# Gate logits from one product with 16 weight columns: rounded weights and their rest side by side, summed after the turn

## What is computed

```python
def _L0_ffn_ref(x, gamma1, Wq, bq, Wdown, bdown, Wup, bup, Wo, bo, gamma2, Wg, bg, We):
    ...
    x = x + (out @ Wo + bo)
    h2 = _rmsnorm(x, gamma2)
    gate = jax.nn.softmax(h2 @ Wg + bg, axis=-1)
    combined = jnp.einsum('btd,edf,bte->btf', h2, We, gate)
    return x + combined
x = L0_attn_hidden_states
x = x + 0.5 * _L0_ffn_ref(_layernorm(x, axis=-1), ...)
x = x + _L0_attn_ref(_layernorm(x, axis=-1), ...)
x = x + 0.5 * _L0_ffn_ref(_layernorm(x, axis=-1), ...)
```

## Time and profile before

| | us |
|---|---|
| median of 3 runs | 1097.27 |
| lowest and highest | 1095.72, 1097.42 |
| the profiled execution | 1095.98 |
| its span in the trace | 1094.1 |
| PE busy | 1030.9 (94%) |
| DVE busy | 872.0 (80%) |
| POOL busy | 726.5 (66%) |
| ACT busy | 653.4 (60%) |

### The profile page before, as it was taken

The page is one execution under the profiler, slowest core; times in us unless marked ns, Lnnn a source line. Parts: engine busy times, 40 slices in busy tenths (PEclk is TensorE's granted clock), DMA queues, the critical chain, the costliest instruction groups (busy, mean ns, idle before and its releaser), DMA issues. The chain is left out here.

```text
span 1094.1 us, 28463 instructions
## 1 busy us (share of the span) xinstructions
PE 1030.9 (94%) x11320; PEld 779.6 (71%) x11320; DVE 872.0 (80%) x1372; ACT 653.4 (60%) x1331; POOL 726.5 (66%) x727
## 2 busy tenths in 40 slices
PE   4799999999999989999999999877999999999997
PEld 3577878888888755666656565456878788788785
DVE  7888788788786379899899999977886777876853
ACT  4565465564665357777777776645655555655642
POOL 8677476576564458787787778983674664755544
PEclk9899999999999999999999999998999999999999
DMA  6210000000000000000000000000000000000000
GB/s 198 69 40 1 1 2 1 2 1 2 2 2 1 2 1 1 2 1 2 1 2 1 2 2 1 2 1 2 2 2 21 21 2 20 22 1 22 21 1 40
DMA packets 8411, 14.30 MB, mean 13 GB/s; under 512 B 2516, under 2 KB 6102, under 8 KB 8280
## 3 DMA queue, kind: packets, MB, share of 16 engines
q1 hardware_dynamic: 8280, 12.47, 3.4%
HBM read 8.28 MB, written 4.19 MB: 11 GB/s over the span
## 5 line engine op out<-in xcount | busy, mean ns | idle before, releaser
L441 PE MATMUL psum<-we,h 128*128 128x512 f32 x1536 | 396.6, 402 | 0.3 <-DVE X L1059 0.3
L441 PEld LDWEIGHTS psum<-we,h 128*128 128x128 f32 x1536 | 275.9, 188 | 59.3 <-issue 2.3
L1237 ACT ACTIVATE late<-psum,gate 128x256 f32<-128x256 f32 x256 | 107.2, 471 | 140.7 <-PE psum L441 96.1
L1413 POOL TENSOR_TENSOR late<-late 128x512 f32<-128x512 f32 x64 | 82.5, 1290 | 147.8 <-ACT late L1237 147.8
L1085 DVE TENSOR_REDUCE oT<-psum 128x128 fp32r<-128x1024 f32 x128 | 155.7, 1219 | 26.3 <-PE psum L808 26.2
L1059 DVE SCALAR_TENSOR_TENSOR X<-psum,gate,X 128x256 f32<-128x256 f32 x256 | 122.8, 480 | 60.1 <-PE psum L441 47.9
L1287 ACT ACTIVATE kvx<-psum 128x1024 f32<-128x1024 f32 x128 | 131.2, 1025 | 65.0 <-PE psum L818 62.5
L1450 POOL TENSOR_TENSOR kvx<-kvx,late 128x2048 f32<-128x2048 f32 x32 | 124.6, 3894 | 42.1 <-ACT late L1294 42.1
L1091 DVE TENSOR_REDUCE late<-kvx 128x256 f32<-128x2048 f32 x64 | 145.7, 2277 | 0.0
L1450 POOL TENSOR_TENSOR late<-kvx,late 128x2048 f32<-128x2048 f32 x32 | 124.5, 3891 | 24.7 <-ACT late L1294 24.7
L818 PE MATMUL psum<-oT,neg_id 128*128 128x512 f32 x256 | 93.8, 447 | 12.6 <-DVE oT L1085 12.1
(11 more groups left out here) (152 smaller groups left out, 1979.0 us busy)
## 6 DMA issues: line engine op xcount, KB each, us to landing
X<-in_L_attn_hidden_states SPq DMA_DIRECT2D x8, 512.0 KB, 5.3
out<-X SPq DMA_DIRECT2D x8, 512.0 KB, 2.6
X<-in_L_ffn_We SPq DMA_DIRECT2D x2, 1024.0 KB, 9.8
kvx<-in_L_ffn_Wq SPq DMA_DIRECT2D x1, 256.0 KB, 3.2
kvx<-in_L_ffn_Wup SPq DMA_DIRECT2D x2, 128.0 KB, 3.1
kvx<-in_L_ffn_Wo SPq DMA_DIRECT2D x1, 256.0 KB, 4.2
X<-in_L_attn_Wk SPq DMA_DIRECT2D x1, 256.0 KB, 2.8
X<-in_L_attn_Wq SPq DMA_DIRECT2D x1, 256.0 KB, 3.5
```

The lines of the kernel that those rows point to most:

```text
L441: ins = e.matmul(out_ap, l, r, start=(n == 0 and not opened), stop=(n == len(terms) - 1), skip_group_check=opened)
L1237: e.activation(y[:, n // 2 * 2 + w, :], psum[:, u % 3, w * D:(w + 1) * D], ACT.Copy, scale=gate[k % 2][:, i, 2 * n + w:2 * n + w + 1]).the ...
L1413: own.step(e.tensor_tensor(y[:, 0:2, :], y[:, 0:2, :], y[:, 2:4, :], ALU.add))
```

## The change

The weights' rounded part and their rest are laid side by side as 16 stationary columns (`wg` is now 128 x KC x 2 x 8). One product of the 16 columns with h2's rounded part and one with h2's rest, for two blocks of features, are four matmuls where six were; the product of rest by rest is computed as well. The result is 16 rows: 8 with the rounded weights, 8 with their rest. gate_copy copies 16 rows; the bias is added to the first 8 and zero to the others, for which POOL clears the bias tile first, and SP waits for that clearing before it loads the bias. gateT turns 16 rows, and gate_sub has one step more: DVE adds the two halves from PSUM into `gl` in SBUF, and maximum and subtraction then read `gl`. In the planner's table two lengths are changed.

```diff
@@ all_steps @@
-            put("PE", size(1400, 720), ("gate", s, w), *(("h2_lo", s, p) for p in own), turned, ("rest_lo", 5))
+            put("PE", size(950, 490), ("gate", s, w), *(("h2_lo", s, p) for p in own), turned, ("rest_lo", 5))
             put("ACT", size(680, 430), ("gate_copy", s, w), ("gate", s, w))
             put("PE", size(300, 200), ("gateT", s, w), ("gate_copy", s, w), last)
-            put("DVE", size(400, 350), ("gate_sub", s, w), ("gateT", s, w))
+            put("DVE", size(650, 600), ("gate_sub", s, w), ("gateT", s, w))
@@ macaron, tiles @@
-        wg = sbt(ctx, "wg", [P, 2, KC, E], F32R)
+        wg = sbt(ctx, "wg", [P, KC, 2, E], F32R)
-        bgate = sbt(ctx, "bgate", [E, 1])
+        bgate = sbt(ctx, "bgate", [2 * E, 1])
-        gT = ct[0:E].rearrange("e g n -> e (g n)")
+        gT = ct[0:2 * E].rearrange("e g n -> e (g n)")
@@ pe_program @@
-                    terms = [(wg[:, y_, kk, :], h2[k % 2][:, x_, kk, cols]) for kk in range(KC) for x_, y_ in THREE]
-                    product(e, psum[0:E, b, cols], terms).then_inc(s_gl, 1)
+                    terms = [(wg[:, kk, :, :].rearrange("p w e -> p (w e)"), h2[k % 2][:, x_, kk, cols]) for kk in range(KC) for x_ in range(2)]
+                    product(e, psum[0:2 * E, b, cols], terms).then_inc(s_gl, 1)
-                        ins = e.transpose(psum[:, b, i * E:(i + 1) * E], gT[:, i * P:(i + 1) * P], ident[0:E, 0:E])
+                        ins = e.transpose(psum[:, b, 2 * i * E:2 * (i + 1) * E], gT[:, i * P:(i + 1) * P], ident[0:2 * E, 0:2 * E])
@@ dve_program, gate_sub @@
-                    pg = psum[:, b, span(tiles, E)].rearrange("p (i e) -> p i e", e=E)
+                    both = psum[:, b, span(tiles, 2 * E)].rearrange("p (i w e) -> p i e w", w=2, e=E)
+                    pg = gl[:, own_t, :]
                     if done(k, piece[2]) > 1:
                         e.wait_ge(s_gate, done(k, piece[2]) - 1)
                     e.wait_ge(s_gTT, done(k, piece[2]))
+                    own.step(e.tensor_reduce(pg, both, AX.X, ALU.add))
+                    e.wait_ge(own.sem, own.n)
                     own.step(e.tensor_reduce(gs[:, 0, own_t], pg, AX.X, ALU.max))
                     e.wait_ge(own.sem, own.n)
-                    e.tensor_tensor(gl[:, own_t, :], pg, gs[:, 0, own_t].unsqueeze(2).to_broadcast([P, n, E]),
+                    e.tensor_tensor(pg, pg, gs[:, 0, own_t].unsqueeze(2).to_broadcast([P, n, E]),
                                     ALU.subtract).then_inc(s_gsub, 1)
@@ act_program @@
-                    split_hi(wg[:, 0], raw_g, l_wg, 16)
+                    split_hi(wg[:, :, 0], raw_g, l_wg, 16)
-                    e.activation(gT[:, cols], psum[0:E, b, cols], ACT.Identity, bias=bgate[:, 0:1]).then_inc(s_gT, 1)
+                    e.activation(gT[:, cols], psum[0:2 * E, b, cols], ACT.Identity, bias=bgate[:, 0:1]).then_inc(s_gT, 1)
@@ pool_program @@
             own.step(e.memset(half_neg[:, :], -0.5))
+            own.step(e.memset(bgate[:, :], 0.0))
             e.memset(ones2f, 1.0).then_inc(s_const, 1)
-                    rest_lo(wg[:, 1], raw_g, wg[:, 0], l_wg, 6)
+                    rest_lo(wg[:, :, 1], raw_g, wg[:, :, 0], l_wg, 6)
@@ sp_program @@
-            e.dma_start(bgate[:, :], a["L0_ffn_bg"].rearrange("(n o) -> n o", o=1)).then_inc(l_bgate, 16)
+            e.wait_ge(s_const, 2)
+            e.dma_start(bgate[0:E, :], a["L0_ffn_bg"].rearrange("(n o) -> n o", o=1)).then_inc(l_bgate, 16)
```

## The result

| | before | after |
|---|---|---|
| median, us | 1097.35 (4 runs) | 1104.45 (4 runs) |
| ratio, 95% interval | | 1.0068 [1.005, 1.0085] |
| a second comparison, us | 1097.34 (15 runs) | 1102.93 (5 runs) |
| its ratio | | 1.0052 [1.0037, 1.0066] |
| span of the profiled execution, us | 1094.1 | 1103.0 |

A forecast was written before the change was run, and what follows sets the result against it. The prediction took TensorE, busy 1030.9 of 1094.1 us (94%), as the bound. Its terms, 0.8 + 2.5 + 1.8 - 1.05 - 1.6 + 0.2 = 2.65 us off the median of 1097.27, gave 1094.6 us, range 1091.0 to 1098.2.

The follow-up runs named there:

- e3: The kernel after, with DVE's halving step in gate_soft taken out and its factor 0.5 put into the last step: 1101.15 us, 1.0030 against the kernel before.
- e4: The kernel after, with ScalarE's exp of the gates put ahead of its copy of turned probabilities: 1102.17 us, 1.0041 against the kernel before.

## What to carry to other kernels

When a short step of DVE moves in time, look up what POOL runs at its new place: here a multiplication or subtraction with its operands in SBUF, begun while POOL's instruction ran, lasted until that ended, however small it was. Its wait is not shown as idle time but inside its own duration. A step whose duration differs between like stages is the sign to look for. Where such a step stands in a chain that PE waits for, fewer steps, an operand in PSUM or a reduction in its place can be worth more than a faster product: here one folded multiplication gave 2.3 us alone, and about 6 with the smaller product, which alone gave none. And lengths in a planner's table are a change of their own: test the new arithmetic in the old order first.

## What the runs showed of the hardware

- A DVE multiplication of 128x4 took 0.17 us beside no POOL instruction and 1.19 us beside a POOL addition of 1.28 us, ending within 0.03 us of it. The next step did the same when the first was gone (1.11 us, e3) or already done (1.27, e4). A step that started 0.01 us before POOL's addition or together with it took 0.17 and 0.19. The reductions and reciprocals of these chains kept 0.18 to 0.19.
- POOL's own instructions grew less: in after, L1418 with 128x512 elements took 1.46 us in the eight cases that ran beside DVE's mask products throughout, and 1.29 on average where none ran.
- One PE wait of 1.16 us in a stage left the granted clock at 1.00. With one of 2.6 to 2.9 us at the attention's start it was 0.55 to 0.79 over the eight us from the first shift, in nine profiles of nine.
- Two executions of the kernel after differ by 2.3 us in the ramps alone (136.0 and 133.7), where PE waits much already.
